# Batch gates folded into copies of the shared down weights, PSUM added straight into the result rows, and a reordered prologue and plan

## The reference

```
mod = (silu(c) @ wmod).reshape(4, 6, 1, 256);  sa, ca, ga, sb, cb, gb = mod[:, 0..5]
ga, gb: sign kept, absolute value at least 0.25
h = layernorm(x) * (1 + ca) + sa
x = x + ga * (softmax(q k^T / sqrt(128)) v) @ w_o       # one head of 128, 2048 keys in each batch
h = layernorm(x) * (1 + cb) + sb
shared = (silu(h @ sg^T) * (h @ su^T)) @ sd^T            # inner width 512
probs = sigmoid(h @ router^T + bias); two best of 8 experts, weights p / sum
routed = sum over the two of  w_e * (silu(h @ gate_e) * (h @ up_e)) @ down_e
out = x + gb * (shared + routed)
```

## Time and profile before

| | us |
|---|---|
| median of 3 runs (lowest to highest) | 1621.56 (1619.24 to 1622.91) |
| the profiled execution's own time | 1623.41 |
| its span | 1621.8 |
| PE busy | 1585.6 |
| DVE busy | 1204.2 |
| ACT busy | 994.4 |
| POOL busy | 528.8 |

### The profile page before, as it was taken

How to read it: one execution, slowest core, us unless ns; L and a number is a source line. 1 busy time by engine, 2 the same in 40 slices (tenths; PEclk the granted TensorE clock), 3 DMA queues, 4 the chain that set the end, 5 groups by cost and what they waited for, 6 DMA issues and landing times.

```text
span 1621.8 us, 37347 instructions
## 1 busy us (share of the span) xinstructions
PE 1585.6 (98%) x12578; PEld 1525.2 (94%) x12579; DVE 1204.2 (74%) x2492; ACT 994.4 (61%) x1735; POOL 528.8 (33%) x597
## 2 busy tenths in 40 slices
PE   8999999999999999999989999999999999999998
PEld 6799999999999998999989999999999999999987
DVE  6678787777778777898776676766666666666687
ACT  5566666666665556666655666666666666666653
POOL 2545445232300001477761222222222222222321
PEclk9999999999999999999999999999999999999999
DMA  3233343111101326322243132133133231111796
GB/s 124 85 117 125 118 143 124 53 46 45 35 27 37 134 111 186 109 96 92 95 149 95 57 104 65 58 110 110 58 98 94 88 107 62 55 61 41 185 268 184
DMA packets 69610, 160.36 MB, mean 99 GB/s; under 512 B 12932, under 2 KB 17924, under 8 KB 68872
## 3 DMA queue, kind: packets, MB, share of 16 engines
q1 hardware_dynamic: 44872, 93.96, 17.4%
q0 software_dynamic: 23248, 62.97, 13.2%
q10 hardware_dynamic: 1392, 2.10, 0.4%
HBM read 90.75 MB, written 68.24 MB: 98 GB/s over the span
## 4 chain that ended last, share of the span: by engine, by line
PE 48%; DVE 6%; DMA 3%; issue 1%; POOL 1%; ACT 1%; POOLq 0%; DVEq 0%; ACTq 0%; SPq 0%
PE f_bank L957 30%; PE f_bank L32 5%; PE f_bank L34 5%; PE f_bank L33 5%; PE f_bank L939 2%; DMA w_all<-y_rows 2%; POOL x_rows L1420 1%; DVE f_prod L1012 1%; DVE f_aT_lo L1004 1%; DMA y_rows<-more_rows,goes_to 1%; DVE xT_lo L1085 1%; PE f_bank L930 1%; DVE more_rows L1053 0%; DVE more_rows L1059 0%; DVE Z L1763 0%
## 5 line engine op out<-in xcount | busy, mean ns | idle before, releaser
L957 PE MATMUL f_bank<-xT_hi,w_cur_hi 128*128 128x256 f32 x1136 | 322.0, 283 | 0.7 <-ACT f_silu_g L992 0.7
L957 PE MATMUL f_bank<-xT_hi,w_cur_lo 128*128 128x256 f32 x1136 | 321.9, 283 | 0.0
L957 PE MATMUL f_bank<-xT_lo,w_cur_hi 128*128 128x256 f32 x1136 | 321.9, 283 | 0.0
L1438 POOL DMA_INDIRECT y_rows<-more_rows,goes_to x142 | 139.0, 979 | 436.1 <-ACT more_rows L1536 250.2
L1917 DVE TENSOR_TENSOR w_cur_lo<-w_all,w_cur_hi 128x1024 fp32r<-128x1024 f32 x142 | 173.5, 1222 | 63.4 <-ACT w_cur_hi L1503 63.4
L1012 DVE TENSOR_TENSOR f_prod<-f_silu_g,f_bank 128x512 f32<-128x512 f32 x206 | 141.6, 687 | 104.2 <-PE f_bank L957 102.5
L957 PEld LDWEIGHTS f_bank<-xT_hi,w_cur_hi 128*128 128x128 f32 x1136 | 218.0, 192 | 0.8 <-issue 0.8
L957 PEld LDWEIGHTS f_bank<-xT_hi,w_cur_lo 128*128 128x128 f32 x1136 | 218.4, 192 | 0.0
L957 PEld LDWEIGHTS f_bank<-xT_lo,w_cur_hi 128*128 128x128 f32 x1136 | 218.2, 192 | 0.0
L957 PE MATMUL f_bank<-xT_hi,w_shared 128*128 128x256 f32 x1024 | 204.1, 287 | 3.8 <-DVE xT_lo L1744 3.3
L418 ACT ACTIVATE prob<-s_pair,negmax 128x1024 f32<-128x1024 f32 x128 | 142.0, 1114 | 90.4 <-DVE negmax L770 90.4
(11 more groups left out here) (295 smaller groups left out, 4392.7 us busy)
## 6 DMA issues: line engine op xcount, KB each, us to landing
more_rows<-x_rows POOLq DMA_DIRECT2D x71, 260.0 KB, 3.0
XS<-in_x SPq DMA_DIRECT2D x32, 256.0 KB, 3.2
XR<-in_x SPq DMA_DIRECT2D x32, 256.0 KB, 2.9
x<-XR SPq DMA_DIRECT2D x32, 256.0 KB, 2.1
Z<-x SPq DMA_DIRECT2D x4, 2048.0 KB, 11.6
w_all<-y_rows SPq DMA_DIRECT2D x32, 256.0 KB, 5.8
w_all<-y_rows POOLq DMA_DIRECT2D x32, 256.0 KB, 7.0
out<-Z SPq DMA_DIRECT2D x31, 256.0 KB, 4.9
```

Source lines behind the costliest of these rows:

```text
L957: mm = pe.matmul(out[:, 2 * P * i:2 * P * i + 2 * P], w, x, start=(c == 0 and n == 0), stop=(c == HC - 1 and n == 2))
L1438: pool.indirect_dma_start(d.y_rows, bass.IndirectOffsetOnAxis(ap=goes_to[:, par, t:t + 1], axis=0), y[:, t, :], None).then_inc(y_sent[t], 16)
```

## The change

- Each of the four batches gets a copy of the shared down matrix, multiplied by its gate row before the split, on POOL, as pieces 2 to 5 of now 14. `w_shared` starts with batch 0's copy; `load_down` brings batch 1's into a new buffer `w_down`, batch 2's over batch 0's, batch 3's over batch 1's. PE waits for the copy at the first tile of each batch.
- `gated`, `add_late`, `gys` and `gy_done` go. `shared_out` adds y from PSUM into Z, and that frees the bank. The routed sum is still multiplied by the gate in `gate_chunk`.
- The chunks of the last stage are taken from 0 to 31; steps 19 to 21 take two each and none is left behind the last step. The last tile's product stands behind its step's chunks, its low part directly behind that.
- Prologue: chunks 2 and on are issued when `cols` has landed; ACT splits `wqkv` before it issues `wo`, the mask and `wmod_rows`.
- End of attention: ACT normalises rows 0 and 1 earlier in the last group.
- Plan: `plan_starts` and all behind it move by one step, as does the split of the first expert.
- A second set of rows moves in SBUF, so ACT waits for the stores of x1 before row 4, and for tile 32's y before the first split. At the last expert step `single_high` stands before two outputs.

The diff, cut to its core (lines of "..." mark what is left out):

```diff
+        FIRST_GATED = 2
+        def of_gated(i):
+            return FIRST_GATED <= i < FIRST_GATED + NB
+        def loads_up_to(i):
+            return 16 * sum(2 if of_gated(k) else 1 for k in range(i + 1))
+        def splits_up_to(i):
+            return sum(3 if of_gated(k) else 2 for k in range(i + 1))
...
+                if of_gated(i):
+                    gate = d.mod_d.rearrange("o (b n) -> o b n", b=NB)[:, i - FIRST_GATED, 3 * H:4 * H]
+                    sp.dma_start(gate_row[:], gate.to_broadcast([P, H])).then_inc(piece_in, 16)
...
-                sp.wait_ge(piece_split, 2 * i + 2)
+                sp.wait_ge(piece_split, splits_up_to(i))
...
-            for m in range(NG + 4):
+            chunk(0)
+            chunk(1)
+            sp.wait_ge(cols_loaded, 16)
+            for m in range(2, NG + 4):
...
-                pool.wait_ge(piece_in, 16 * i + 16)
+                pool.wait_ge(piece_in, loads_up_to(i))
+                if of_gated(i):
+                    by_chunk = piece_raw[:].rearrange("p (c h) -> p c h", h=H)
+                    pool.tensor_tensor(by_chunk, by_chunk, gate_row[:].unsqueeze(1).to_broadcast([P, W // H, H]),
+                                       ALU.mult).then_inc(piece_split, 1)
+                    pool.wait_ge(piece_split, splits_up_to(i) - 2)
...
-                pool.wait_ge(piece_split, 2 * i + 1)
+                pool.wait_ge(piece_split, splits_up_to(i) - 1)
...
+            act.wait_ge(w_loaded, 16)
+            act.activation(w_hi[:], w_raw, ACT.Copy).then_inc(w_split, 1)
+            act.dma_start(wo_raw, wo).then_inc(wo_loaded, 16)
+            act.dma_start(mask_i[:], mask).then_inc(wo_loaded, 16)
...
-            act.dma_start(wo_raw, wo).then_inc(wo_loaded, 16)
-            act.dma_start(mask_i[:], mask).then_inc(wo_loaded, 16)
-            act.wait_ge(w_loaded, 16)
-            act.activation(w_hi[:], w_raw, ACT.Copy).then_inc(w_split, 1)
...
+                if G == ALL - 1:
+                    normalise_rows(act, d, 0)
...
+                if G == ALL - 1:
+                    normalise_rows(act, d, 1)
...
-                if G == ALL - 1:
-                    for m in range(2):
-                        normalise_rows(act, d, m)
...
-    FIRST = 4
-    chunk_order, chunks_of = [], []
-    resting = iter(range((ALL + FIRST) // C))
+    chunks_of, k = [], 0
...
-        chunks_of.append([])
-        goal = len(chunk_order) + (0 if i < 4 else 1 if i % 2 and i > 9 else 2)
-        if i >= FIRST + 4 and i % 2 == 0:
-            chunks_of[i].append((ALL + i - 4) // C)
-        while len(chunk_order) + len(chunks_of[i]) < goal:
-            chunks_of[i].append(next(resting))
-        first = len(chunk_order)
-        chunk_order += chunks_of[i]
-        chunks_of[i] = list(range(first, len(chunk_order)))
-    assert len(chunk_order) == CHUNKS - 2
-    chunk_order += [CHUNKS - 1, CHUNKS - 2]
-    assert sorted(chunk_order) == list(range(CHUNKS))
+        n = 0 if i < 4 else 1 if i % 2 and 9 < i < LATE - 3 else 2
+        chunks_of.append(range(k, k + n))
+        k += n
+    assert k == CHUNKS
...
-                                             for part, o in ((spare, 4 * W), (more, 0), (more, SLOT))]
-        early_norm, early_vt, early_gys = (of_two(spare[:, SLOT + 2 * H * k:SLOT + 2 * H * k + 2 * H]) for k in range(3))
-        assert SLOT + 6 * H <= 4 * W
-        gys = [early_gys, of_two(more[:, 0:2 * H])]
+                                             for part, o in ((spare, SLOT + 4 * H), (more, 0), (more, SLOT))]
+        early_norm, early_vt = (of_two(spare[:, SLOT + 2 * H * k:SLOT + 2 * H * k + 2 * H]) for k in range(2))
+        assert 2 * SLOT + 4 * H + 2 * W <= 8 * W
...
+        other_down = columns_of(d.w_down, W, 0, H)
...
-        SPLIT_AT = STEPS + 6
+        SPLIT_AT = STEPS + 7
...
+        def batch_of(m):
+            return tile_of(m) // TB
...
-                src = d.raw[e][part] if o < 2 * W else d.w_parts[(3 + e) // 3, :, part, W * ((3 + e) % 3):W * ((3 + e) % 3) + W]
+                i = d.first_down + e
+                src = d.raw[e][part] if o < 2 * W else d.w_parts[i // 3, :, part, W * (i % 3):W * (i % 3) + W]
...
+            def load_down(b):
+                i = 2 + b
+                sp.wait_ge(d.shared_ready, 16 * b)
+                if b % 2:
+                    to = d.w_down[:].rearrange("p (a n) -> p a n", a=2)
+                else:
+                    to = d.w_shared[:].rearrange("p (a n) -> p a n", a=2)[:, :, 2 * W:3 * W]
+                sp.dma_start(to.bitcast(F32), d.w_parts[i // 3, :, :, W * (i % 3):W * (i % 3) + W]
+                             ).then_inc(d.shared_ready, 16)
...
+            load_down(1)
+            sp.wait_ge(f.y_mm, TB)
+            load_down(2)
...
-            sp.wait_ge(gy_done, ALL)
-            sp.wait_ge(sent[0], ONCE * (GROUPS // RING))
+            sp.wait_ge(f.y_out, ALL)
+            for i in range(2):
+                sp.wait_ge(sent[i], ONCE * (GROUPS // RING))
...
-                n = C * chunk_order[k]
+                n = C * k
...
+            sp.wait_ge(f.up_mm, L0)
+            load_down(3)
...
-            for k in range(CHUNKS):
-                if k == CHUNKS - 2:
-                    continue
+            for k in range(CHUNKS - 1):
+                n = C * k
...
-                n = C * chunk_order[k]
+                sp.wait_ge(f.y_out, max(ALL, n + C))
...
-            n = C * chunk_order[CHUNKS - 2]
+            n = C * (CHUNKS - 1)
+            sp.wait_ge(out_done, CHUNKS)
...
-                sp.wait_ge(gy_done, ALL + FIRST + t + 1)
+                sp.wait_ge(f.y_out, n + t + 1)
...
+                if m == GS:
+                    for semaphore, value in d.x1_stored:
+                        act.wait_ge(semaphore, value)
+                    act.wait_ge(d.stats1_done, NT)
...
+                    act.wait_ge(f.y_mm, 2 * TB)
...
+                if not inside(j + 1, NP):
+                    single_high(d.extra + 1)
...
-                if not inside(j + 1, NP):
-                    single_high(d.extra + 1)
...
+            def shared_of(m):
+                return shared_weights[0:2] + [other_down if batch_of(m) % 2 else shared_weights[2]]
...
+                if tile_of(m) % TB == 0:
+                    pe.wait_ge(d.shared_ready, 16 * batch_of(m) + 16)
...
-                    f.pe_pair_down(pe, t, (home(m), home(m + 1)), shared_weights)
+                    f.pe_pair_down(pe, t, (home(m), home(m + 1)), shared_of(m))
...
-            def gated(m):
+            chunks_added = []
+            def shared_out(m):
...
-                if m == 0:
-                    dve.wait_ge(gate_loaded, 80)
-                dve.tensor_tensor(gys[m >= L0][:, m % 2, :], f.y_bank[m % 2][:, 0:H], rows[:, tile_of(m) // TB, 0:H],
-                                  ALU.mult).then_inc(f.y_out, 1)
-            def shared_out(m):
-                dve.wait_ge(f.y_out, shared_count(m))
+                k = tile_of(m) // C
+                if k in chunks_added:
+                    dve.wait_ge(out_done, k + 1)
...
-                dve.tensor_tensor(z, gys[m >= L0][:, m % 2, :], z, ALU.add).then_inc(gy_done, 1)
+                dve.tensor_tensor(z, f.y_bank[m % 2][:, 0:H], z, ALU.add).then_inc(f.y_out, 1)
...
+                if k == 0:
+                    dve.wait_ge(gate_loaded, 80)
...
-                c = chunk_order[k]
-                if ALL + FIRST <= C * c < NT - C:
-                    dve.wait_ge(f.y_out, shared_count(L0 + C * c + C - 1 - ALL))
-                gate = rows[:, C * c // TB, 0:H].unsqueeze(1).to_broadcast([P, C, H])
+                gate = rows[:, C * k // TB, 0:H].unsqueeze(1).to_broadcast([P, C, H])
...
-            def output_chunk(k):
-                n = C * chunk_order[k]
+            def output_chunk(k, tiles_added):
+                n = C * k
...
-                dve.wait_ge(gy_done, min(ALL + FIRST, max(ALL, n + C)))
+                dve.wait_ge(f.y_out, min(tiles_added, n + C))
...
-            def add_late(i):
-                k = chunk_order.index((ALL + i) // C)
-                m = L0 + i
-                dve.wait_ge(f.y_mm, m + 1)
-                dve.wait_ge(y_sum[k % SLOTS], 16 * (k // SLOTS + 1))
-                part = slots[:, k % SLOTS, (ALL + i) % C, :]
-                dve.tensor_tensor(part, f.y_bank[m % 2][:, 0:H], part, ALU.add).then_inc(f.y_out, 1)
+                chunks_added.append(k)
...
-                if n >= 3:
-                    gated(n - 3)
...
                     plan_ends()
+                if n == STEPS + 4:
                     plan_starts()
-                if n == STEPS + 4:
                     plan_behind()
+                if n == STEPS + 5:
                     plan_experts()
-                if n == STEPS + 5:
+                if n == STEPS + 6:
                     plan_moves()
...
-                    gated(ALL - 3)
...
-                        gated(ALL - 2 + t)
...
-                if 3 <= i < 3 + FIRST:
```

(20 more changed lines are left out.)

11 lines of the change are left out of this document (6 added, 5 removed).

## The result

The kernel after takes 1612.10 us (median of three runs, 1610.59 to 1612.66), the kernel before 1621.56: a ratio of 0.9937, 95% interval 0.9923 to 0.9951. Forecast were 1614.8, in a range of 1611.0 to 1619.5. The profiled execution took 1612.66 (span 1611.1), 10.75 less than that of before; the sum of the prediction was 6.8.

What follows compares the result with a forecast made beforehand. TensorE (PE), busy 98% of the span, was taken to bound the kernel. Terms 0.9 + 3.3 - 1.7 + 4.1 + 0.2 = 6.8 us gave 1614.8 us against the median of 1621.56; range 1611.0 to 1619.5.

Steps and rivals of the forecast that it cites:

- Prologue, 0.9: Program start: less x data issued ahead lets `cols` land earlier; 0.9 us gained, bounds 0 and 1.5.
- The upper bound: Prologue: PE's clock could rise before its 3.54 us of work on `cols` are through, up to 1.8 us more.
- Routed stage, 3.3: Up to placing group 6: fewer DVE instructions remove PE's seven `xT_lo` waits, 3.0 us; with earlier placing 3.3.
- POOL's chain, 0: Placing to first expert: POOL's 32 indirect transfers, shortened by no edit, bound the first block; the plan's edit gains 0.
- the clock, -1.7: First expert block: PE idles 3.4 us, its clock falls to half, costing 1.7 us; bounds 0 and 1.7.
- the first rival: First expert: no low clock, so the forecast without the 1.7 us loss, 1613.1 us; chance 0.18.
- Four gated copies, 0: POOL's multiplications of 128x1024, 2.4 us each, are hidden in its waits; cost 0.
- Last stage, 4.1: Up to tile 54: half clock gone, one new wait of 1.5 at step 9; net 4.1 us gained, bounds 1.5 and 5.4.
- the slower rival: Last stage: `load_down(3)` delays the loads of y, making the kernel 3.0 us slower, 1624.6 us; chance 0.08.
- Tail, 0.2: Program end: one `gated` less, 0.53, minus 0.35 for a later bank release; 0.2 us gained, bounds -0.7 and +1.5.

Runs made afterwards that it cites:

- e1: Kernel after, with chunk 2 of x issued at once instead of behind the landing of `cols`: 1609.81 us, kernel before on that chip 1620.73.
- e12: Kernel after, with ACT's split of `wqkv` again behind the issue of `wo`, the mask and `wmod_rows`: 1715.55 us, kernel before on that chip 1709.38.
- e6: Kernel after, plus an unused DVE multiplication of y from PSUM by the gate for tiles 0-31 and late tiles 0-19: 1738.74 us, ratio to before 1.0088.
- e10: The kernel of e6 unchanged, run later on the same chip: 1715.99 us, kernel before there 1709.38.
- e5: Kernel after, DVE writing `aT_lo` behind a last-stage step's first chunk, and adding tile 61's y before the last product: 1719.60 us, ratio to before 0.9994.
- e4: Kernel after, with PE's transposes of the first expert block behind the down product of tiles 38 and 39: 1607.22 us, ratio to before 0.9915.

## Why the prediction was right, and where its terms were off

The time lay in the range and on the side forecast, 2.7 us below the point. The two large terms, routed and last stage, hold; two small ones came out by luck, and one was wrong. By its steps:

- *Prologue, 0.9.* Measured 0.75, by two effects that are not in the sum. `cols` was there 1.3 earlier, but in this execution 0.5 was lost again between the keys and v_lo, where a stretch of low clock stands from 22.8 to 26.2 us. That the two together come near 0.9 is luck. Chunk 2 is the part that counts (e1), the new order of ACT's queue is not (e12). The upper bound, that the clock could rise before the o_bank matmuls are through, was not a property of the edit: it happens or not from one execution to the next, for 3.2 us.
- *Routed stage, 3.3.* Measured 4.2 up to the placing of group 6 (with 0.1 from the end of attention). The size was taken from the seven waits that the view lists, 3.0. At six of these, of 0.45 to 0.50, PE's transposes gain 0.34 to 0.42, since 0.1 is left. But they gain 0.25 to 0.31 also two tiles ahead of each, where the idle time was 0.10 to 0.17 and but one wait is listed. That DVE's two instructions fewer bring it is read from the traces; the experiments meant to test it (e6, e10) could not.
- *POOL's chain, 0, and the clock, -1.7.* This is the step that failed. I let the chain of 32 scatters pass as one "that no edit shortens". Its length hangs on what DVE does beside it: it shrank by 1.8. Counted from the placing, PE gained 2.6 ahead of the block, where 1.9 were reckoned (2.2 less 0.3), so the wait was 1.5 + 2.6 - 1.8 = 2.28 and not 3.4. The clock stayed at 1.00, and the first rival, "no low clock", is the one that came true (1613.1, against 1612.1). But the shorter wait is not shown to be the reason. A fixed 1.7 for a wait above 2.5 was itself wrong: the same wait of 2.73 for v_lo was followed by 0.50 in eight of fourteen executions and not in six, so the term is a matter of chance.
- *Four gated copies, 0.* As predicted: the multiplications take 2.40 each, as the subtraction does, all in the shade of the attention, and the last piece is split at 331.7.
- *Last stage, 4.1.* Measured 4.07. The walk holds in the main: the product is 3.70 ahead at tile 7 and 3.89 at tile 8 (1537.73 against 1548.14, less the 6.52 that were ahead at tile 3), where 3.7 was named for tile 8; the half clock is gone, and there is a new wait, 1.26 at 1537.53, a step earlier than the 1.5 that was named for step 9. The wait of 1.25 at 1548.05 is not new; the kernel before has it at the same tile:

```profile
1558.56 0.39 PE L32 MATMUL f_bank<-w_shared,f_aT_hi 128*128 128x256 f32 x1 [1.25 <-DVE f_aT_lo L1004]
```

DVE waits for no y but the first (1.20 at 1518.41, before 1.51); `load_down(3)`, issued at 1495.32, did not hold the loads of y up (first issue 1507.88), so the slower rival had nothing to stand on.
- *Tail, 0.2.* Measured 0.18, which is luck: from the product of tile 19 to the last y seven executions of this code take 16.9 to 18.7 us, the kernel before 17.85. It is made of two parts much larger than thought: the chunks that now stand ahead of the last products put them 1.4 and 1.5 later, and the end without `gated` and without the left chunk gave 3.1 back. e5 shows that the first was avoidable.

The sum: 0.75 + 4.17 + 1.80 - 0.20 + 4.07 + 0.18 = 10.77. Against it the forecast of 6.8 was 4.0 short, 3.5 of it in the two entries on POOL's chain and the clock.

## What to carry to other kernels

A chain on another engine that "nothing touches" has to be checked against what runs beside it: GpSimd's scatters here lengthen by up to 0.8 us when they begin inside a vector instruction that reads two SBUF operands, and never when it reads one from PSUM. That moving an operand to PSUM shortens such a chain as a whole is shown here for 0.3 us only. Where PE waits for something late, look at what is queued behind the wait and ready; two moves of order (e4, e5) shortened the segments by 9 to 10 us together, nearly as much as this whole change; that the program's time follows was shown for neither. A cost of the clock that one trace shows behind one wait is a chance and not a term. And before a difference of 2 us is believed, compare the segments: the start of this kernel alone differs by 3.2 us between executions of the same instructions.

## What the runs showed of the hardware

- The issue of an indirect transfer by POOL (0.96 us) that starts inside a vector TENSOR_TENSOR with two SBUF sources ends no earlier than 0.83 to 0.86 behind that instruction's end (all 69 long ones of the two kernels' traces, 348 of all fourteen). Four that began with the vector instruction, within 0.02 us of its start, took 0.96 all the same. Inside an instruction with a source in PSUM none lasted over 1.0 (340 cases).
- The time at which PE reaches its higher rate differs between executions of the same code: the clock's first record at 1.00 begins at 5.8 to 6.6 us in eight of the fourteen and at 12.6 to 16.0 in six, and the 16 small matmuls from 6.3 us on take 1.92 to 2.08 us or 3.55.
- The same wait of PE, 2.73 us for v_lo, is followed by a granted clock of 0.50 in eight executions and leaves it at 1.00 in six. Three waits of 2.28 to 2.38 left it at 1.00; one of 2.49 in the kernel before was followed by 0.50.
- A load on SP's queue that is under way beside one of ACT's delays it: `cols` landed at 7.26 us with a third chunk of x beside it, at 6.14 to 6.84 without.
- On two of the three chips of the experiments the same programs stand for up to 15 us (PE) or 19 (DVE, ACT) at a time while POOL issues scatters, 100 us in all. What these stops are is not known.
